# Attention, experts and feed-forward in one kernel: the parts of the row maxima move from VectorE to GpSimd in the plain attention stage

## The chip, the cores and the metric

One Trainium2 chip, one core. The metric is the device time of one execution in microseconds. The time of before is the median of three executions. One further execution was recorded by the hardware profiler; all rows below are from it.

## The reference

The kernel computes two layers on x of shape 8 x 512 x 256 with a context of the same shape, in this order (cut to what matters):

```python
x = x + L0_xattn(ctx, ctx, layernorm(x), mask, ...)   # 16 heads of 16, plain (mask only), then Wo
x = x + L0_ffn(layernorm(x), ...)                     # layer norm, causal attention of 16 heads, then
                                                      # 8 experts of 256 -> 1024 -> 256, the best 2 per token
x = x + L1_xattn(layernorm(x), ctx, ...)              # one head of 256, no mask
x = x + L1_ffn(layernorm(x), ...)                     # silu(gate) * up, integer weights times 1/127
```

In both attentions of 16 heads: scores = q k^T, p = softmax(scores), out = p v.

## The kernel before, in words

The work runs in seven phases with a barrier of all engines between them: `phase_first` (projections of the plain attention), `phase_attention` with causal False, `phase_second` (output projection, projections of the causal attention), `phase_attention` with causal True, the gates, the experts, and the last layer. The change touches the first four, one number in the experts' phase, and no arithmetic of the result.

`phase_attention` works on 32 units G: a batch has 16 heads, and a unit is four of them. Operands are split into a high and a low half of 16 bits, which share the contraction. For a unit, PE makes the scores once (`score`, L953), VectorE takes the row maxima from them (`top`, L1092, eight reductions a unit in the plain stage), and the negated maxima are added as further rows of the operands when PE makes the scores a second time, transposed (`shifted`, L975). ScalarE takes the exponent (L1072), PE weighs the values (`weigh`, L991), and VectorE divides (`normalise`, L1114 and L1116). The scores of unit G + 2 are made while unit G is in its second pass.

How the maxima reach the operands: VectorE makes their high and low parts in 16 bits (`shift`, L1103 and L1106), PE transposes them (`turn`, L1003, at step 8 of 16 of the unit before), ScalarE copies the row out (`shift_rows`, L1060), SyncE moves it into the operand with two DMAs (L885), and the unit's first product waits for these.

Heads are loaded by half batches (two units) into four slots; a load (`heads.load`, L189 and L191) is five DMAs, or four without a mask, and each half batch takes two loads. FIRST_LOADS = 2 half batches are loaded by the projection phases, the next two early in the attention ("late"), the others one load a unit.

Beside the plain attention, GpSimd splits 22 weight pieces (`prep`) into high and low halves: 16 of 2048 columns a lane, 3 of 512, 3 of 1536 (integers). Raw pieces and results have two buffers each. SyncE loads a raw piece (`raw_load`, L893) and stores a result (`pair_store`, L898); GpSimd scales (L867), takes the high half (L872) and the low half (L875). Ahead of the high half it waits for the store that last used the buffer:

```python
if i >= 2:
    pool.wait_ge(pair_out[i % 2], 16 * (i // 2))     # line 871
pool.tensor_copy(pair[:, HIGH], raw)                 # line 872
```

All DMAs of this phase are issued by SyncE in program order. Its turn G begins with the two rows of unit G + 1, for which it waits for ScalarE's copy; then come the late loads, the load of heads, the store of split G - 2 (line 919) and the raw load of split G (line 921). In the causal stage two of its turns load an expert's weights (L924) in two DMAs of 1 MB.

Of the kernel before, what the change touches and what calls it, by code (L numbers as in the profile page):

```python
# [12 lines left out]
ALU = mybir.AluOpType  # L13
# [4 lines left out]
P = 128  # L18
B, S, D = 8, 512, 256
TT = S // P  # L20
# [5 lines left out]
G_ALL = B * NG  # L26
EPS = 1e-5
NEG = -1e30
E_N, FF = 8, 1024
# [79 lines left out]
NSC = 1024.0  # L109
PRODUCTS = ((0, 0), (0, 1), (1, 0))  # L110
LOW, HIGH = 1, 0
# [81 lines left out]


LOADS0, LOADS1 = 10, 8
FIRST_LOADS = 2


def phase_first(nc, c, w, scr, vall, heads, pk, w16):
# [544 lines left out]
def phase_attention(nc, c, causal, scr, vall, oall, heads, extra, spare, prep):  # L744
# [3 lines left out]
    NP_BUF, NE, NM_BUF = 24 if causal else 12, 3, 4  # L748
    K6, Q6, ident, identh, idm, cmq, cmk = (heads.k, heads.q, heads.ident, heads.identh, heads.idm, heads.cmq,
                                            heads.cmk)  # L750
    nm = [c.sb(f"nm{s}", [P, TT, 2, 2]) for s in range(NM_BUF)]
    nparts = [c.sb(f"nparts{s}", [P, TT * 2, 2, 2], F16) for s in range(2)]
# [10 lines left out]
    qk, mask = scr["qk"], scr["mask"]  # L763
# [7 lines left out]
    if causal:  # L771
        masked = c.sem("masked")
    else:
        mask_set, pair_ready, prep_own = c.sem("mask_set"), c.sem("pair_ready"), c.sem("prep_own")
        raw_in, pair_out = ([c.sem(f"{n}{p}") for p in range(2)] for n in ("raw_in", "pair_out"))
        buffers = Arena(spare)
        raws = [buffers.take([P, 2048]) for _ in range(2)]
        prepared = [buffers.take([P, 2, 2048], F16) for _ in range(2)]
        assert len(prep) < G_ALL - 1

    def prob_of(unit):
        return prob[unit % NP_BUF // 4][:, unit % 4]
# [17 lines left out]
    NPAIR = len(pairs)  # L800
# [29 lines left out]
    with nc.Block() as block:  # L830

        @block.gpsimd
        def _(pool):
            if causal:
                for G in range(G_ALL):
                    for t in range(TT):
                        own = [k for k, u in enumerate(units) if u[0] == t]
                        heads_in, w = len(units[own[0]][1]), e_width(t)
                        at = (G * NU + own[0]) % NP_BUF
                        diagonal = (prob[at // 4][:, at % 4:at % 4 + len(own), 0:heads_in * w]  # L840
                                    .rearrange("p k (h n) -> p k h n", h=heads_in)[:, :, :, 0:P])
                        pool.wait_ge(p_ready, G * NU + own[-1] + 1)
                        pool.affine_select(out=diagonal, in_=diagonal, compare_op=ALU.is_ge, fill=0.0, base=0,  # L843
                                           pattern=[[0, len(own)], [0, heads_in], [1, P]], channel_multiplier=-1
                                           ).then_inc(masked, 1)
                return
            pool.memset(idm[:], 0.0).then_inc(mask_set, 1)
            pool.memset(cmq[:], 0.0).then_inc(mask_set, 1)
            pool.memset(cmk[:], 0.0).then_inc(mask_set, 1)
            pool.wait_ge(mask_set, 3)  # L850
            for v in range(3):
                at = (v - 1) * RT
                pool.affine_select(out=idm[:, v, :], in_=idm[:, v, :], compare_op=ALU.not_equal, fill=MC, base=at,
                                   pattern=[[-1, P]], channel_multiplier=1)
                pool.affine_select(out=cmq[:, v, :], in_=cmq[:, v, :], compare_op=ALU.is_ge, fill=-MC, base=at,
                                   pattern=[[-1, P]], channel_multiplier=1)
                pool.affine_select(out=cmk[:, v, :], in_=cmk[:, v, :], compare_op=ALU.is_ge, fill=-MC, base=-at,
                                   pattern=[[1, P]], channel_multiplier=-1)
            steps = 0
            for i, (src, n, dst, scale, integer) in enumerate(prep):  # L860
                raw, pair = raws[i % 2][:, 0:n], prepared[i % 2][:, :, 0:n]
                pool.wait_ge(raw_in[i % 2], 16 * (i // 2 + 1))
                if integer:
                    pool.tensor_copy(raw, raw.bitcast(I32)).then_inc(prep_own, 1)
                    steps += 1
                    pool.wait_ge(prep_own, steps)
                pool.tensor_scalar(raw, raw, scale, None, ALU.mult).then_inc(prep_own, 1)  # L867
                steps += 1
                pool.wait_ge(prep_own, steps)
                if i >= 2:  # L870
                    pool.wait_ge(pair_out[i % 2], 16 * (i // 2))
                pool.tensor_copy(pair[:, HIGH], raw).then_inc(prep_own, 1)  # L872
                steps += 1
                pool.wait_ge(prep_own, steps)
                pool.tensor_tensor(pair[:, LOW], raw, pair[:, HIGH], ALU.subtract).then_inc(pair_ready, 1)  # L875

        @block.sync
        def _(sp):
# [9 lines left out]
            def raw_load(i):  # L888
                src, n, dst, scale, integer = prep[i]
                if i >= 2:  # L890
                    sp.wait_ge(pair_ready, i - 1)
                raw = raws[i % 2][:, 0:n].rearrange("p (c f) -> p c f", c=src.shape[1])
                sp.dma_start(raw.bitcast(I32) if integer else raw, src).then_inc(raw_in[i % 2], 16)  # L893
# [11 lines left out]
            for G in range(G_ALL):  # L905
                if G + 1 < G_ALL:
                    shift_rows(G + 1)
                if G == 0:
                    heads.load(sp, *late[0], qk, mask)
                    heads.load(sp, *late[1], qk, mask)  # L910
                elif G <= 2:
                    heads.load(sp, *late[G + 1], qk, mask)
                if G >= 2 and G // 2 + SLOTS - 1 < NHB:
                    if G % 2 == 0:
                        sp.wait_ge(p_ready, G * NU)
                    heads.load(sp, G // 2 + SLOTS - 1, G % 2, qk, mask)
                if not causal:
                    if 2 <= G < len(prep) + 2:
                        pair_store(G - 2)
                    if 2 <= G < len(prep):  # L920
                        raw_load(G)
                elif G in (4, 6):
                    k = (G - 4) // 2
                    sp.dma_start(scr["ew_to"][:, 5, k], scr["ew"][5, k]).then_inc(scr["ew_in"], 16)  # L924
            if not causal:
                for p in range(2):
                    sp.wait_ge(pair_out[p], 16 * ((len(prep) + 1 - p) // 2))
# [151 lines left out]
        def _(dve):  # L1079
# [42 lines left out]
            for G in range(LA):  # L1122
                for p in range(NPAIR):
                    top(G, p)
                    if G == 1 and p < 2:
                        shift(0, p)
            for G in range(G_ALL):
                for p in range(NPAIR):
                    if G + LA < G_ALL:
                        top(G + LA, p)  # L1130
                    if p < 2 and G + 1 < G_ALL:
                        shift(G + 1, p)
                    if p == EARLY - 1 and G > 0:
                        normalise(G - 1)
# [359 lines left out]
def phase_experts(nc, c, scr, ew_to, ew_in, slots, hist, ones, xs_out):  # L1494
# [49 lines left out]
    with nc.Block() as block:  # L1544
# [173 lines left out]
        def _(pe):  # L1718
# [40 lines left out]
                    last.then_inc(y_ps, 1)  # L1759

            pe.wait_ge(map_ready, 2)
            pe.wait_ge(ew_in, 16 * 2 * E_N)
            transpose(0, 0)

            def expert_of(s):
# [817 lines left out]
```

## Time and profile before

| what | us |
|---|---|
| median of three executions | 2091.76 (2085.29 to 2096.83) |
| the profiled execution | 2095.28 |
| its span, first to last instruction | 2093.5 |
| PE busy in the span | 1770.4 |
| VectorE busy | 1332.8 |
| ScalarE busy | 1098.2 |
| GpSimd busy | 570.9 |

The span is what the profiler recorded between the first and the last instruction; the time of the execution is a little longer. A busy time is a sum over the whole span, and the phases have different limits, so shares are read by stretches. In the rows, PE is TensorE's matmul, PEld its weight load, DVE is VectorE, ACT ScalarE, POOL GpSimd, and SPq SyncE issuing a DMA. L1103 is line 1103 of the kernel before.

### The profile page before, as it was taken

To read this page: it belongs to the slowest core of one execution; us is meant where nothing else is said; L and a number is where in the kernel's file an instruction comes from. 1 tells how busy PE (TensorE), PEld (TensorE's weight loads), DVE (VectorE), ACT (ScalarE), POOL (GpSimd) and SP (SyncE) were. 2 spreads that over 40 slices of the span, in tenths; PEclk is the share of its full clock that TensorE was granted. 3 is DMA by queue.
4 is the path that set the end of the run, shared out by engine and by line. 5 is a ranking of instruction groups with operands and counts; after the bars stand their busy time and mean duration, and the time that the engine had idled before them with its cause. 6 is when DMAs were issued, how large, how long until landed. Compare 5 with 4: busy or idle time off the path is not lost. (4 is left out here: it accounts for less than half of the span.)

```text
span 2093.5 us, 40227 instructions
## 1 busy us (share of the span) xinstructions
PE 1770.4 (85%) x13889; PEld 1078.1 (51%) x13890; DVE 1332.8 (64%) x2426; ACT 1098.2 (52%) x2041; POOL 570.9 (27%) x479
## 2 busy tenths in 40 slices
PE   7668888999896889997675599999998469989987
PEld 4312222222673444444564488888887245556555
DVE  6478898996565668883575455555454367767753
ACT  6336777878452567775441244444443246546551
POOL 5244899510430223332366000000000422222000
PEclk9869999999997899998675799999999689999999
DMA  6524665410341121113322211111111411111000
GB/s 186 154 87 140 211 197 179 139 65 2 111 125 60 50 81 49 49 35 130 136 102 82 71 51 45 45 46 50 45 45 41 173 41 51 51 52 50 21 11 21
DMA packets 103208, 171.74 MB, mean 82 GB/s; under 512 B 16008, under 2 KB 78368, under 8 KB 98976
## 3 DMA queue, kind: packets, MB, share of 16 engines
q1 hardware_dynamic: 96928, 153.19, 22.9%
q0 software_dynamic: 6144, 16.79, 2.5%
q8 instruction: 80, 1.31, 0.3%
q14 instruction: 56, 0.46, 0.1%
HBM read 103.34 MB, written 61.87 MB: 79 GB/s over the span
## 5 line engine op out<-in xcount | busy, mean ns | idle before, releaser
L1092 DVE TENSOR_REDUCE a_nm<-a_psS 128x2 f32<-128x1024 f32 (+1 forms) x384 | 446.9, 1191 | 51.4 <-PE a_psS L953 38.3
L1072 ACT ACTIVATE a_prob<-a_psE 128x512 f32<-128x512 f32 (+2 forms) x660 | 335.2, 563 | 122.1 <-PE a_psE L975 120.5
L975 PE MATMUL a_psE<-wall 51*128 51x512 f16 (+3 forms) x1024 | 291.7, 359 | 38.1 <-DMA wall<-a_nrow 26.9
L953 PE MATMUL a_psS<-wall 49*128 49x512 f16 (+4 forms) x1024 | 268.2, 369 | 35.3 <-DVE a_nm L1092 22.6
L1710 ACT ACTIVATE ex_hf<-ex_psH,ex_b 128x256 f32<-128x256 f32 x312 | 130.7, 470 | 216.4 <-PE ex_psH L1741 216.4
L1741 PE MATMUL ex_psH<-ex_xT,wall 128*128 128x256 f16 x1872 | 232.1, 274 | 7.5 <-issue 4.1
L1755 PE MATMUL ex_psY<-wall,ex_hl 128*128 x1872 | 229.8, 273 | 1.4 <-DVEq L1661 0.4
L975 PEld LDWEIGHTS a_psE<-wall 51*128 51x128 f16 x1024 | 76.8, 95 | 276.1 <-ACT a_prob L1072 106.5
L1741 PEld LDWEIGHTS ex_psH<-ex_xT,wall 128*128 x1872 | 182.4, 98 | 34.7 <-issue 13.0
L1755 PEld LDWEIGHTS ex_psY<-wall,ex_hl 128*128 128x128 f16 x1872 | 179.3, 98 | 31.9 <-issue 10.9
L1672 DVE CAST ex_hl<-ex_hf 128x512 f16<-128x512 f32 x156 | 66.6, 427 | 182.2 <-ACT ex_hf L1710 180.4
L991 PE MATMUL a_psO<-a_prob,wall 128*32 128x512 f32 (+3 forms) x1576 | 171.2, 523 | 2.5 <-ACT a_prob L1072 0.7
L1072 ACT ACTIVATE wall<-a_psE 128x512 f32<-128x512 f32 x236 | 128.1, 604 | 42.7 <-PE a_psE L975 42.2
L1949 POOL MEMSET la_identh<- 128x128 f16 x1 | 0.2, 205 | 466.6 <-POOLq L2502 466.6
L867 POOL TENSOR_SCALAR xall<-xall 128x2048 f32<-128x2048 f32 (+2 forms) x22 | 102.6, 4664 | 72.7 <-DMA xall<-in_w 58.5
L843 POOL TENSOR_SCALAR_AFFINE_SELECT a_prob<-a_prob 128x512 f32<-128x512 f32 x112 | 73.5, 656 | 176.7 <-ACT a_prob L1072 176.6
L953 PEld LDWEIGHTS a_psS<-wall 49*128 49x128 f16 (+1 forms) x1024 | 70.6, 96 | 90.5 <-DVE a_nm L1092 57.8
L1673 DVE TENSOR_TENSOR ex_hl<-ex_hf,ex_hl 128x512 f16<-128x512 f32 x156 | 108.1, 693 | 5.4
L1088 DVE TENSOR_REDUCE a_nm<-a_psS 128x4 f32<-128x1024 f32 x64 | 61.2, 958 | 64.0 <-PE a_psS L961 64.0
L1972 POOL TENSOR_TENSOR la_var<-la_mv,la_eps 128x4 f32<-128x4 f32 x16 | 8.5, 533 | 315.2 <-DVE la_mv L2004 315.2
L961 PE MATMUL a_psS<-wall 64*128 64x128 f16 x1024 | 88.7, 229 | 0.0
L2336 PE MATMUL la_psG<-la_yT,la_wgate 128*128 128x512 f16 x288 | 72.5, 389 | 11.7 <-ACT la_yT L2215 11.7
(282 smaller groups left out, 3160.0 us busy)
## 6 DMA issues: line engine op xcount, KB each, us to landing
s_qk<-wall SPq DMA_DIRECT2D x32, 512.0 KB, 3.2
wall<-s_qk SPq DMA_DIRECT2D x128, 128.0 KB
xall<-in_w SPq DMA_DIRECT2D x16, 1024.0 KB, 11.8
s_ew<-xall SPq DMA_DIRECT2D x16, 1024.0 KB, 9.2
wall<-s_ew SPq DMA_DIRECT2D x16, 1024.0 KB, 10.6
ex_xt<-s_xs SPq DMA_DIRECT2D x39, 256.0 KB, 2.6
s_ys<-ex_yo SPq DMA_DIRECT2D x39, 256.0 KB, 2.2
t_xin<-in_x SPq DMA_DIRECT2D x16, 512.0 KB, 5.2
```

Of the source, the lines that this page charges most:

```text
L843: pool.affine_select(out=diagonal, in_=diagonal, compare_op=ALU.is_ge, fill=0.0, base=0, pattern=[[0, len(own)], [0, heads_in], [1, P]], c ...
L867: pool.tensor_scalar(raw, raw, scale, None, ALU.mult).then_inc(prep_own, 1)
L953: last = pe.matmul(psS[:, bank, col:col + n], Q6[s][at:at + SROWS, pr, t * P:(t + 1) * P], K6[s][at:at + SROWS, pr, 0:n], start=True, stop ...
L961: last = pe.matmul(psS[:, banks(use) + x, col + t * P:col + n], idm[at:at + RT, u + 1 - x, :], cmq[at:at + RT, u + 1 - x, :], start=False, ...
L975: last = pe.matmul(psE[unit % NE][:, col:col + w], K6[s][at:at + EROWS, pr, t * P:(t + 1) * P], Q6[s][at:at + EROWS, pr, S - w:S], start=T ...
L991: last = pe.matmul(psO[c4 * HP:(c4 + 1) * HP, S - w:S], vall[:, at:at + HP], prob_of(G * NU + k)[:, col:col + w], start=t == 0, stop=t == ...
L1072: act.activation(prob_of(unit)[:, 0:w], psE[unit % NE][:, 0:w], ACT.Exp, scale=ESC).then_inc(p_ready, 1)
L1092: dve.tensor_reduce(nm[G % NM_BUF][:, t, :, i], psS[:, at:at + 2, 0:n], axis=AX.X, op=ALU.max, negate=True).then_inc(s_free, 1)
L1673: dve.tensor_tensor(hl[q][:, 1, two, :], hf[:, two, :], hl[q][:, 0, two, :], ALU.subtract).then_inc(hl_ready, 1)
L1710: act.activation(hf[:, f, :], psH[f // 2][:, f % 2, :], ACT.Gelu_apprx_tanh, bias=b1[q][:, f:f + 1], scale=1.0 / (WSCALE * XSCALE)).then_i ...
L1741: last = pe.matmul(psH[f][:, j, :], ew_to[:, ds(e, 1), 0, wp, at:at + P].rearrange("p o f -> p (o f)"), xT[q][:, xp, d, :], start=n == 0, ...
L1755: last = pe.matmul(psY[t][:, 0:D], hl[q][:, hp, fc, t * P:(t + 1) * P], ew_to[:, ds(e, 1), 1, wp, fc * D:(fc + 1) * D].rearrange("p o d -> ...
```

## The change

In the plain stage the two instructions of `shift` leave VectorE. GpSimd makes the parts with three instructions (scale by 1/1024 into a new tile `nscaled`, copy to 16 bits, subtract), in the order parts of unit 0, then for each split i: parts of unit i + 1, split i; then the parts of the units left. The causal stage keeps `shift` on VectorE. FIRST_LOADS goes from 2 to 3, so that one half batch is loaded late in place of two: its two loads are issued in turns 0 and 1. The raw load of split G + 1 is issued in turn G, one turn earlier than before; the store of split G - 2 stays in turn G. In the causal stage the expert's weights are loaded in eight pieces of 256 KB, one a turn from 4 to 11, and the experts' phase waits for the new count.

```diff
-FIRST_LOADS = 2
+FIRST_LOADS = 3
...
             steps = 0
+
+            def shift_parts(G):
+                nonlocal steps
+                src = nm[G % NM_BUF][:].rearrange("p t x i -> p (t x) i")
+                dst = nparts[G % 2]
+                pool.wait_ge(s_free, (G + 1) * NPAIR)
+                pool.tensor_scalar(nscaled[:], src, 1.0 / NSC, None, ALU.mult).then_inc(prep_own, 1)
+                steps += 1
+                pool.wait_ge(prep_own, steps)
+                if G >= 2:
+                    pool.wait_ge(nT_ps, G - 1)
+                pool.tensor_copy(dst[:, :, HIGH], nscaled[:]).then_inc(prep_own, 1)
+                steps += 1
+                pool.wait_ge(prep_own, steps)
+                pool.tensor_tensor(dst[:, :, LOW], nscaled[:], dst[:, :, HIGH], ALU.subtract).then_inc(nparts_ready, 1)
+
+            shift_parts(0)
             for i, (src, n, dst, scale, integer) in enumerate(prep):
+                shift_parts(i + 1)
                 raw, pair = raws[i % 2][:, 0:n], prepared[i % 2][:, :, 0:n]
                 pool.wait_ge(raw_in[i % 2], 16 * (i // 2 + 1))
...
+            for G in range(len(prep) + 1, G_ALL):
+                shift_parts(G)
...
-                if G == 0:
-                    heads.load(sp, *late[0], qk, mask)
-                    heads.load(sp, *late[1], qk, mask)
-                elif G <= 2:
-                    heads.load(sp, *late[G + 1], qk, mask)
+                if G < len(late):
+                    heads.load(sp, *late[G], qk, mask)
...
                     if 2 <= G < len(prep) + 2:
                         pair_store(G - 2)
-                    if 2 <= G < len(prep):
-                        raw_load(G)
-                elif G in (4, 6):
-                    k = (G - 4) // 2
-                    sp.dma_start(scr["ew_to"][:, 5, k], scr["ew"][5, k]).then_inc(scr["ew_in"], 16)
+                    if 2 <= G + 1 < len(prep):
+                        raw_load(G + 1)
+                elif 4 <= G < 12:
+                    k, half, part = (G - 4) // 4, (G - 4) // 2 % 2, slice((G - 4) % 2 * 1024, (G - 4) % 2 * 1024 + 1024)
+                    sp.dma_start(scr["ew_to"][:, 5, k, half, part], scr["ew"][5, k, :, half, part]
+                                 ).then_inc(scr["ew_in"], 16)
...
-                    if G == 1 and p < 2:
+                    if causal and G == 1 and p < 2:
                         shift(0, p)
...
-                    if p < 2 and G + 1 < G_ALL:
+                    if causal and p < 2 and G + 1 < G_ALL:
                         shift(G + 1, p)
...
-            pe.wait_ge(ew_in, 16 * 2 * E_N)
+            pe.wait_ge(ew_in, 16 * (2 * (E_N - 1) + 8))
```

## Rows read from the trace of the kernel before

**Rows 1.** Busy time by stretch: start:end, length, busy of each engine, clock, DMA.
```profile
200.00:300.00 100.00, 85.33 (x595) 22.90 (x594) 90.96 (x101) 78.07 (x149) 91.80 (x25) 1.00 0.63 202
447.00:458.00 11.00, 10.60 (x77) 2.82 (x74) 10.40 (x13) 9.57 (x20) 0.00 (x0) 1.00 0.12 42
```

**Rows 2.** Timeline of ScalarE, row copies of the plain stage: start, length, instruction.
```profile
178.85 0.56 ACT L1060 COPY a_nrow<-a_psS 8x512 f16<-8x512 f16 x1
199.54 0.57 ACT L1060 COPY a_nrow<-a_psS 8x512 f16<-8x512 f16 x1 [0.89 <-PE a_psS L1003]
...
348.09 0.57 ACT L1060 COPY a_nrow<-a_psS 8x512 f16<-8x512 f16 x1 [0.88 <-PE a_psS L1003]
...
421.43 0.57 ACT L1060 COPY a_nrow<-a_psS 8x512 f16<-8x512 f16 x1 [0.40 <-PE a_psS L1003]
...
447.56 0.56 ACT L1060 COPY a_nrow<-a_psS 8x512 f16<-8x512 f16 x1
...
512.52 0.56 ACT L1060 COPY a_nrow<-a_psS 8x512 f16<-8x512 f16 x1
```

**Rows 3.** Timeline of VectorE: the high parts beside GpSimd's work, and without it.
```profile
232.59 2.29 DVE L1103 TENSOR_SCALAR a_nparts<-a_nm 128x16 f16<-128x16 f32 x1
...
465.83 0.16 DVE L1103 TENSOR_SCALAR a_nparts<-a_nm 128x16 f16<-128x16 f32 x1
```

**Rows 4.** Timeline of GpSimd: one split of 2048 columns, part of one of 512.
```profile
229.49 5.37 POOL L867 TENSOR_SCALAR xall<-xall 128x2048 f32<-128x2048 f32 x1 [1.56 <-DMA xall<-in_w]
234.92 1.93 POOL L872 CAST xall<-xall 128x2048 f16<-128x2048 f32 x1
236.93 4.08 POOL L875 TENSOR_TENSOR xall<-xall 128x2048 f16<-128x2048 f32 x1
...
365.12 0.61 POOL L872 CAST xall<-xall 128x512 f16<-128x512 f32 x1
365.81 1.16 POOL L875 TENSOR_TENSOR xall<-xall 128x512 f16<-128x512 f32 x1
```

**Rows 5.** Timeline of all engines: from a unit's transposes to the store.
```profile
236.28 0.39 PE L1003 MATMUL a_psS<-wall,a_nparts 128*8 128x128 f16 x4 [0.71 <-DVE a_nm L1092]
...
236.70 0.57 ACT L1060 COPY a_nrow<-a_psS 8x512 f16<-8x512 f16 x1 [0.50 <-PE a_psS L1003]
...
237.30 1.33 SPq L885 DMA_DIRECT2D wall<-a_nrow  x2
...
238.67 2.15 SPq L189 DMA_DIRECT2D wall<-s_qk  x4
...
241.54 0.44 SPq L898 DMA_DIRECT2D s_ew<-xall  x1
```

**Rows 6.** DMAs: landing of all 22 stores, one of 1 MB, those of 256 KB.
```profile
DMA to landing us min/median/max: 6.7/9.1/15.3
...
s_ew<-xall SPq DMA_DIRECT2D x1, 1024.0 KB, 10.8
...
s_lw<-xall SPq DMA_DIRECT2D x3, 256.0 KB, 6.9
```

**Rows 7.** Timelines of SyncE and GpSimd: the first raw loads and the first split.
```profile
133.28 0.92 SPq L893 DMA_DIRECT2D xall<-in_w  x2
...
138.36 5.39 POOL L867 TENSOR_SCALAR xall<-xall 128x2048 f32<-128x2048 f32 x1 [17.59 <-DMA xall<-in_w]
```

**Rows 8.** Busy time by stretch, behind a long wait; columns as in rows 1.
```profile
192.00:193.00 1.00, 1.00 (x8) 0.20 (x8) 1.00 (x2) 1.00 (x3) 1.00 (x1) 0.50 0.12 45
```

**Rows 9.** Timelines of ScalarE and PE in the causal stage: row copies, one wait.
```profile
681.34 0.57 ACT L1060 COPY a_nrow<-a_psS 8x512 f16<-8x512 f16 x1 [1.33 <-PE a_psS L1003]
...
721.11 0.39 PE L975 MATMUL a_psE<-wall 51*128 51x512 f16 x1 [4.00 <-DMA wall<-a_nrow]
...
770.23 0.57 ACT L1060 COPY a_nrow<-a_psS 8x512 f16<-8x512 f16 x1 [0.26 <-PE a_psS L1003]
778.80 0.57 ACT L1060 COPY a_nrow<-a_psS 8x512 f16<-8x512 f16 x1 [0.18 <-PE a_psS L1003]
```

More of the change, by code:

```diff
@@ L773, in phase_attention @@
     else:
+        nscaled = c.sb("nscaled", [P, TT * 2, 2])
         mask_set, pair_ready, prep_own = c.sem("mask_set"), c.sem("pair_ready"), c.sem("prep_own")
@@ L778, in phase_attention @@
         prepared = [buffers.take([P, 2, 2048], F16) for _ in range(2)]
-        assert len(prep) < G_ALL - 1
+        assert len(prep) < G_ALL - 3
     def prob_of(unit):
```

## The prediction

> **What bounds the kernel now.** I read the busy shares by stretch first, then the row copies of ScalarE as a clock of the units, then the timelines of one unit, and last the times to landing. The plain attention stage is about a fifth of the span. While GpSimd splits weights beside it, VectorE is 91% busy and GpSimd 92%; late in the stage, with GpSimd silent, PE is busy 10.60 of 11.00 us and VectorE 10.40 [rows 1]. One copy of a row (L1060) marks each unit: the last six steps are (512.52 - 447.56) / 6 = 10.83 us, while from 199.54 to 348.09 twelve steps take 12.38 us each, and one step takes 20.7 us [rows 2]. From 178.85 to 512.52 there are 27 steps in 333.7 us; at 10.83 they would take 292.4. So some 41 us lie above the floor that PE sets, and that is all the change can win here.
>
> A good part of the 41 us has a visible cause. L1103, which makes the high parts of the maxima on VectorE, takes 2.29 us at 232.59 and ends at 234.88, 0.02 us after GpSimd's L867 ends; with GpSimd silent it takes 0.16 us [rows 3, 4]. VectorE is held by GpSimd's long instructions.
>
> **The change, part by part: what VectorE loses.** Two instructions a unit, 0.33 us where nothing holds them, 2.5 us where L867 does [rows 3]. That is a gain only if nothing later takes its place, since without the hold the unit is PE's 10.83 us [rows 1, 2].
>
> **What GpSimd gets.** Three instructions a unit on 16 values a lane. No row shows them. From 512 to 2048 columns L872 grows from 0.61 to 1.93 us and L875 from 1.16 to 4.08, so both begin near 0.18 us [rows 4]; with 16 columns I take 0.22 each and 0.2 us for the gaps of three linked steps, 0.85 us a unit. The bounds are 0.5 (begin alone, no gaps) and 2.0 (each 0.61, as the dearest near row, with gaps); below nothing they can't be, as each is an instruction in the loop named next. A split of 2048 columns takes 11.52 us (229.49 to 241.01), so GpSimd alone needs 12.35 us a unit, already the pace of before.
>
> **What the order of GpSimd's work ties together.** This is the step that decides. Before, GpSimd's splits and the units of attention met nowhere. Now GpSimd runs parts(i+1), split i, parts(i+2), split i+1, and so on. Split i holds a wait that the diff leaves as it is: from i = 2 on, ahead of its L872, it waits until the store of split i-2 has landed (line 871), because that buffer is written again. SyncE issues that store in its turn G = i (line 919), after the shift rows of unit i+1, which wait for the row copy, which waits for the transposes, which wait for parts(i+1). So the store, which was 10 us ahead of need, is now issued only once parts(i+1) is made, and parts(i+2) can't be made until it has landed. Queued behind GpSimd's wait are its own L872, L875 and parts(i+2); waiting for those are PE's transposes of unit i+2 and with them everything of the attention.
>
> The price of one turn round this loop, from one unit of before [rows 5]: the transposes start, 0.42 us later the copy, 0.60 us later SyncE's first row; with 0.08 us for GpSimd's signal that is 1.10. From the first row to the store is 241.54 - 237.30 = 4.24 us, in which two rows, four head loads and a mask are issued. The store lands 9.1 us after issue, the median of 22, 16 of them of 1 MB and nearly all behind the same head loads [rows 6]. Then L872 and L875, 234.92 to 241.01, 6.09 us [rows 4], and the parts, 0.85. Sum 1.10 + 4.24 + 9.1 + 6.09 + 0.85 = 21.4 us a unit, against 12.4 before. Ends for the landing: 6.9 us (the stores of 256 KB) and 10.8 us (the slowest 1 MB store once the stage is running; the 15.3 was an early one, behind doubled head loads), so 19.2 to 23.1 us [rows 6]. I take 9.1, since the same transfers stand ahead of the store.
>
> The raw load goes out one turn earlier and is no shorter path: issued right behind the store, it is needed a whole turn later.
>
> **How many turns.** I number the row copies from 0 (178.85 is number 4, 199.54 number 5, 348.09 number 17, 421.43 number 23) [rows 2]. Copy i+2 follows copy i+1 by the loop of split i. Number 4 is late already, because the first looped store goes out after copy 3: GpSimd starts split 0 at 138.36, when its raw data is in [rows 7], and two splits with their parts later, 2 x 12.37, parts 3 are made at 163.1; copy 3 is then at about 165, the first looped store 4.8 us behind it, its landing 9 to 12 us, and 8.0 us for the rest, so 187 against 178.85. Splits 3 to 15: 13 x 21.4 = 278.2. Splits 16 and 17 have 512 columns (1.85 us in place of 6.09 [rows 4]) behind 1 MB stores: 2 x 17.2. Split 18 behind a 256 KB store: 15.0. Splits 19 and 20, 1536 columns (4.6 us, between the two) behind 6.9 us: 2 x 17.7. Split 21 behind 768 KB, 8.4 us between the two: 19.2 [rows 6]. Together 382.2, so copy 23 at 569 us against 421.43: 148 us late. The eight steps left take 8 x 10.83 = 86.6 against 91.1, with 1 us for a clock to recover: after a long wait PE was granted half its clock (0.50, that is 1.2 of 2.4 GHz) for some microseconds [rows 8]. The stage: 148 - 4.5 + 1 = +145 us. Inside the loop the half clock costs little, since PE has 21 us for work that takes 10.8.
>
> **Three half batches loaded early.** Both projection stages issue two more head loads (L189, 2.15 us and some 0.6 for a mask [rows 5]). The first lies in a queue that waits anyway, the last beside the landing of the final store; 0 to 1 us each, +1 in all. GpSimd's and SyncE's other steps aren't moved past.
>
> **The causal stage.** VectorE keeps its parts there. Its floor is 778.80 - 770.23 = 8.57 us a unit; from copy 681.34 to 770.23 there are eight steps in 88.9 us, 20.3 above the floor. Four waits of PE for a row that stood in the queue (the longest 4.00 us) come to 12.1, and what follows each wait is PE at less than full clock [rows 9]. Doubled head loads and two 1 MB loads of expert 5 stand ahead of those rows; after the change each turn has one head load, and the expert's 2 MB goes in eight pieces of 256 KB. Gain between 0 (the bytes are the same) and 20.3; I take 14, the waits and a little of their wake.
>
> **Sum.** The profiled execution took 2095.3 us (span 2093.5, with 1.8 around it), 3.5 above the median of 2091.8. 2095.3 + 145 + 1 - 14 = 2227 us.
>
> **The rivals.** (1) Slower by less, a short landing. The queue is emptier when units take longer, so the store may land as the first raw load did in an empty queue: issued at 133.28, used at 138.36, 5.1 us [rows 7]. The loop is then 17.4 us; 15 turns lose 4.0 each and the six short ones some 1.5: 2227 - 69 = 2158. Against it: the head loads are still issued 3 us ahead of every store, and a 256 KB store with them ahead still took 6.9. The Trainium skill, page "DMA: Bandwidth & Descriptors", section "Anatomy of one DMA — SWDGE (gpsimd) path", is on this rival's side: about 2.0 us plus the bytes over 436 GB/s, 4.4 us for 1 MB, by which the time would be an estimated 2140 us. It is given for another issue path, and the trace of before disagrees, with 9.1.
> (2) Faster, GpSimd's own pace. If the stores have landed whenever GpSimd reaches L872, the loop has no DMA in it, GpSimd needs 12.35 us a unit and VectorE's holds are gone. Parts 2 are made at 150.7 [rows 7], and copy 17 comes at 150.7 + 15 x 12.35 + 1.1 = 337 in place of 348, the three short splits run at 10.83, the three of 1536 at 11.05, the rest at 10.83: the last copy at 490 against 512.5, so 2095 - 23 - 14 + 1 = 2059. It decides if a store can land within about 5.4 us (L867) of the parts being made; the issue alone comes 5.3 us after them.
> (3) No difference: the parts are ready as early as before because GpSimd has room, the units stay at 12.4 us, and the causal gain is at its low end: 2085 to 2105. The 92% of GpSimd speaks against it [rows 1].
>
> **How the numbers follow.** Forecast (loop over the landing) 0.87; rival 1 0.05; rival 2 0.06; rival 3 0.02. Within the forecast the landing's ends move 15 turns by -33 or +26 us, GpSimd's small steps 21 turns by -7 or +24, and the causal stage by -6 or +14. All at one end would be 2181 to 2291; as the three don't hang together I take the landing's end with half of the others: 2187 to 2272. That leaves out the rivals, 0.13, and thin ends. Faster by over 0.5% 0.06, within 0.5% 0.02, slower 0.92; 0.5% is about what a measurement of this kernel can tell from no change.
>
> **What would show it.** Row copies of the plain stage some 21 us apart from number 4 to 17 and 10.8 from 24 on; GpSimd idle before L872 for about 9 us a unit, ended by the DMA of a store; no idle time of note before L867; PE waiting before L1003 for GpSimd, and its clock falling to half in each unit; VectorE's L1103 gone there, with reductions never over 1.3 us; the causal stage with 8.6 us steps from its fourth unit. GpSimd's three small steps near 0.85 us. The prediction is wrong if GpSimd is not idle before L872, or if copies come 12 to 15 us apart.

## The result, and the profile after

The changed kernel takes 2218.44 us (median of four runs, 2217.67 to 2218.91), the kernel before 2093.98 in the same comparison: a ratio of 1.060, 95% interval 1.057 to 1.064. The prediction said 2227, range 2187 to 2272, and slower. The profiled execution took 2218.91 us, its span is 2217.2 against 2093.5, so 123.7 us are to be found. A time below is the median of a kernel's executions on its chip, or its only one; some executions of a kernel take over 1.5% longer than its fastest, and the ratios, and the median of label e3_loads_alone, leave these out.

Timeline of ScalarE of the changed kernel, the row copies (now L1079): start, length, instruction, idle time before and what ended it. They answer to [rows 2].

```profile
167.01 0.56 ACT L1079 COPY a_nrow<-a_psS 8x512 f16<-8x512 f16 x1
188.63 0.57 ACT L1079 COPY a_nrow<-a_psS 8x512 f16<-8x512 f16 x1 [10.68 <-PE a_psS L1022]
...
470.88 0.57 ACT L1079 COPY a_nrow<-a_psS 8x512 f16<-8x512 f16 x1 [9.17 <-PE a_psS L1022]
...
576.07 0.57 ACT L1079 COPY a_nrow<-a_psS 8x512 f16<-8x512 f16 x1 [6.34 <-PE a_psS L1022]
...
642.24 0.56 ACT L1079 COPY a_nrow<-a_psS 8x512 f16<-8x512 f16 x1
653.07 0.56 ACT L1079 COPY a_nrow<-a_psS 8x512 f16<-8x512 f16 x1
663.89 0.56 ACT L1079 COPY a_nrow<-a_psS 8x512 f16<-8x512 f16 x1
```

The first two rows are copies 3 and 4, the third is copy 17, the fourth copy 23. From 4 to 17 thirteen steps take 282.25 us, 21.71 each, where twelve of the same steps took 12.4 each in [rows 2]; at the end the step is 10.82, as before. The units in between wait for GpSimd, and GpSimd waits for a DMA.

Timeline of GpSimd over one turn of the changed kernel (L867 to L875 are now the parts of the maxima; L886, L891 and L894 are the split's scaling, high and low halves).

```profile
274.86 5.36 POOL L886 TENSOR_SCALAR xall<-xall 128x2048 f32<-128x2048 f32 x1
289.53 1.89 POOL L891 CAST xall<-xall 128x2048 f16<-128x2048 f32 x1 [9.31 <-DMA s_ew<-xall]
291.51 4.05 POOL L894 TENSOR_TENSOR xall<-xall 128x2048 f16<-128x2048 f32 x1
295.53 0.25 POOL L867 TENSOR_SCALAR a_nscaled<-a_nm 128x16 f32<-128x16 f32 x1
295.85 0.20 POOL L872 CAST a_nparts<-a_nscaled 128x16 f16<-128x16 f32 x1
296.13 0.22 POOL L875 TENSOR_TENSOR a_nparts<-a_nscaled,a_nparts 128x16 f16<-128x16 f32 x1
```

Timelines of PE, ScalarE and SyncE over the same turn: transposes, row copy, rows, head loads, mask, store, raw load, and the next copy. They answer to [rows 5].

```profile
275.03 0.58 PE L1022 MATMUL a_psS<-wall,a_nparts 128*8 128x128 f16 x4 [9.29 <-POOL a_nparts L875]
...
275.65 0.57 ACT L1079 COPY a_nrow<-a_psS 8x512 f16<-8x512 f16 x1 [9.01 <-PE a_psS L1022]
...
276.25 1.33 SPq L906 DMA_DIRECT2D wall<-a_nrow  x2
277.62 2.15 SPq L189 DMA_DIRECT2D wall<-s_qk  x4
279.82 0.62 SPq L191 DMA_DIRECT2D wall<-s_mask  x1
280.49 0.44 SPq L919 DMA_DIRECT2D s_ew<-xall  x1
280.97 0.43 SPq L914 DMA_DIRECT2D xall<-in_w  x1
...
297.12 0.57 ACT L1079 COPY a_nrow<-a_psS 8x512 f16<-8x512 f16 x1 [9.29 <-PE a_psS L1022]
```

This is the loop, closed: copy at 275.65, first row 0.60 later, store 4.24 us after that, landed 9.04 us after its issue (289.53), 6.0 us of split, 0.82 us of parts, and 0.77 to the next copy at 297.12, 21.47 us after the last one. GpSimd stands for 9.31 us with an input that was ready.

Waits of the changed kernel in its plain stage (what was waited for: us in total, times, longest):

```profile
PE a_psS L1022 <- POOL a_nparts L875: 162.2, 20, 11.0
POOL xall L891 <- DMA s_ew<-xall: 154.6, 16, 13.2
```

Twenty waits of PE for GpSimd hold 162 us; 16 waits of GpSimd for a 1 MB store hold 155. The second makes the first.

Busy time by stretch of the changed kernel within the same turn (start:end, length, busy of PE, weight load, VectorE, ScalarE and GpSimd, clock, DMA share, GB/s); it answers to [rows 1, 8].

```profile
281.00:288.00 7.00, 5.84 (x43) 1.23 (x36) 6.73 (x6) 6.17 (x12) 0.00 (x0) 1.00 0.88 311
288.00:289.00 1.00, 0.00 (x0) 0.00 (x0) 0.22 (x1) 0.00 (x0) 0.00 (x0) 0.85 0.17 70
289.00:290.00 1.00, 0.00 (x0) 0.00 (x0) 0.00 (x0) 0.00 (x0) 0.47 (x1) 0.50 0.13 53
290.00:295.00 5.00, 0.00 (x0) 0.00 (x0) 0.00 (x0) 0.00 (x0) 4.91 (x2) 0.50 0.03 14
```

PE idles and is granted half its clock (0.50, 1.2 of 2.4 GHz) behind that. In the last microseconds before the store is in, all that moves has a DMA share of 0.13 to 0.17, what two to three of the 16 engines make up. That row became the best lead of the study.

Where the 123.7 us went, from first and last row copies of each stage: 2.3 up to the plain stage's first copy (131.25 to 133.53), 149.1 within that stage (381.3 to 530.4), 0.5 between the stages, -17.7 in the causal stage (286.3 to 268.6), and -10.5 behind it (1135.2 to 1124.7), in code that the change doesn't touch.

### The profile page after: what moved, and what is told of

Read it like the earlier page. It is cut to its first block and busy times, and to the rows that moved or that the text cites. A ratio compares the mean times of both kernels' runs of the same rounds, so it can differ in the third digit from the quotient of the medians.

```text
span 2217.2 us, 40269 instructions
## 1 busy us (share of the span) xinstructions
PE 1779.2 (80%) x13889; PEld 1077.5 (49%) x13890; DVE 1303.8 (59%) x2362; ACT 1094.1 (49%) x2041; POOL 589.5 (27%) x575
## 5 line engine op out<-in xcount | busy, mean ns | idle before, releaser
L1111 DVE TENSOR_REDUCE a_nm<-a_psS 128x2 f32<-128x1024 f32 (+1 forms) x384 | 438.9, 1174 | 59.8 <-PE a_psS L972 50.2
L972 PE MATMUL a_psS<-wall 49*128 49x512 f16 (+4 forms) x1024 | 283.5, 375 | 31.9 <-DVE a_nm L1111 15.6
L1774 PEld LDWEIGHTS ex_psY<-wall,ex_hl 128*128 128x128 f16 x1872 | 179.9, 98 | 31.2 <-issue 10.8
L1022 PE MATMUL a_psS<-wall,a_nparts 128*8 128x128 f16 x256 | 29.3, 248 | 174.2 <-POOL a_nparts L875 162.2
L1133 DVE RECIPROCAL a_rc<-a_psS 128x16 f32<-128x16 f32 x64 | 16.4, 256 | 212.0 <-PE a_psS L1030 212.0
L1079 ACT COPY a_nrow<-a_psS 8x512 f16<-8x512 f16 x64 | 36.5, 571 | 199.7 <-PE a_psS L1022 199.1
L1022 PEld LDWEIGHTS a_psS<-wall,a_nparts 128*8 128x8 f16 x256 | 15.7, 93 | 194.7 <-issue 172.6
L886 POOL TENSOR_SCALAR xall<-xall 128x2048 f32<-128x2048 f32 (+2 forms) x22 | 102.5, 4659 | 7.2 <-DMA xall<-in_w 6.7
## 6 DMA issues: line engine op xcount, KB each, us to landing
wall<-s_ew SPq DMA_DIRECT2D x14, 1024.0 KB, 10.2
```

The lines of the kernel that those rows point to most:

```text
L972: last = pe.matmul(psS[:, bank, col:col + n], Q6[s][at:at + SROWS, pr, t * P:(t + 1) * P], K6[s][at:at + SROWS, pr, 0:n], start=True, stop ...
L1111: dve.tensor_reduce(nm[G % NM_BUF][:, t, :, i], psS[:, at:at + 2, 0:n], axis=AX.X, op=ALU.max, negate=True).then_inc(s_free, 1)
L1774: last = pe.matmul(psY[t][:, 0:D], hl[q][:, hp, fc, t * P:(t + 1) * P], ew_to[:, ds(e, 1), 1, wp, fc * D:(fc + 1) * D].rearrange("p o d -> ...
```

## The experiments

My theory: the loop that the prediction describes sets the unit. Against it, (A) GpSimd simply has too much to do, and (B) the DMA queue is full, so that it matters little who waits for what. The first four kernels below, and the changed kernel with the head loads split, ran once each; they differ from the changed kernel (2217.67 to 2218.91 us) by 78 us and more.

**The store one turn earlier.** SyncE stores split G-1 in turn G, so nothing that GpSimd waits for hangs on the parts that it has just made.

```diff
-                    if 2 <= G < len(prep) + 2:
-                        pair_store(G - 2)
+                    if 1 <= G < len(prep) + 1:
+                        pair_store(G - 1)
```

> The changed kernel with one edit: the store of split G-1 is issued in turn G (before: of split G-2), so that the store which split i waits for goes out one row copy earlier. Theory (the loop over the landing of the store): the wait ahead of GpSimd's high half is gone, and the next late thing is the raw load: row copy to raw issue 5 us, landing 11, a split 11.5, parts 0.9, together some 29.6 us for two units, 14.8 a unit in place of 21.7; total about 2092 us (2080 to 2110), GpSimd idle before its scaling instead of before its high half. Rival A (GpSimd is simply too slow at the parts beside the splits): units stay near 21 us, total over 2190. Rival B (the rows wait in the DMA queue): unchanged within 20 us, since the same bytes are moved.

Measured 2097.75 us, within the range. Copies come in turn 12.3 to 13.7 and 16.0 to 17.7 us apart, some 15 in the mean. Timeline of GpSimd of this kernel, the scaling of one split, and its waits in the plain stage:

```profile
293.46 5.37 POOL L886 TENSOR_SCALAR xall<-xall 128x2048 f32<-128x2048 f32 x1 [5.50 <-DMA xall<-in_w]
```

```profile
POOL xall L886 <- DMA xall<-in_w: 42.5, 12, 8.3
```

No wait for a store is left, and 120 us are back. What is late next is the raw load, which lands 11.5 us after issue.

**Four result buffers in place of two.** No DMA changes its place; GpSimd waits for the store of split i-4 (the buffers and their counts go from two to four throughout; cut here to the wait).

```diff
-                if i >= 2:
-                    pool.wait_ge(pair_out[i % 2], 16 * (i // 2))
+                if i >= 4:
+                    pool.wait_ge(pair_out[i % 4], 16 * (i // 4))
...
```

> The changed kernel with four result buffers in place of two: split i waits for the store of split i-4, issued two turns earlier; no DMA is moved. Theory (loop over the landing): the same as with the store one turn earlier, 14.8 us a unit, total about 2092 us (2080 to 2110), within 10 us of that run. Rivals A and B: 2190 or more.

Measured 2096.09 us, steps of 16.2 and 13.4 us in turn. The same gain with every transfer where it was: it was the dependence that cost the time. The full queue (B) alone would have left the time where it was.

**Store and raw load ahead of the head loads.** The loop stays, the store's place changes.

```diff
                 if G + 1 < G_ALL:
                     shift_rows(G + 1)
+                if not causal:
+                    if 2 <= G < len(prep) + 2:
+                        pair_store(G - 2)
+                    if 2 <= G + 1 < len(prep):
+                        raw_load(G + 1)
                 if G < len(late):
                     heads.load(sp, *late[G], qk, mask)
...
-                if not causal:
-                    if 2 <= G < len(prep) + 2:
-                        pair_store(G - 2)
-                    if 2 <= G + 1 < len(prep):
-                        raw_load(G + 1)
```

> The changed kernel with SyncE's turn in another order: rows, store, raw load, and only then the loads of heads; the store stays in its turn. Theory (loop): the store is issued 2.8 us earlier in the loop and no head loads stand ahead of it, so that it lands in 5 to 7.5 us in place of 9.0; units of 15 to 17.5 us, total about 2100 us (2075 to 2150). If the landing does not depend on the head loads, units of 18.9 us and about 2162 us. Rivals A and B: no change.

Measured 2092.91 us, units of 14.2 to 14.8, a little under the 15 to 17.5 expected. DMAs of this kernel (transfer, count, KB each, median us from issue to landing):

```profile
s_ew<-xall SPq DMA_DIRECT2D x16, 1024.0 KB, 5.0
```

The landing falls from 9.1 to 5.0 us, with the raw load still issued right behind the store. So some 4 us of the landing belonged to what stood ahead. The Trainium skill, page "DMA: Bandwidth & Descriptors", section "Anatomy of one DMA — SWDGE (gpsimd) path", gives about 2.0 us plus the bytes over 436 GB/s for DMAs that GpSimd issues, an estimated 4.4 us for 1 MB. These stores are issued by SyncE, and the trace comes near that figure (5.0) only where no head load stands ahead of the store.

**The raw load one turn later,** as in the kernel before.

```diff
-                    if 2 <= G + 1 < len(prep):
-                        raw_load(G + 1)
+                    if 2 <= G < len(prep):
+                        raw_load(G)
```

> The changed kernel with the raw load of split G in turn G, as before the change. Theory (whatever SyncE issues behind a row copy and GpSimd needs before the next parts is in the loop): the raw load joins it: 1.4 us to the row, 4.7 to the raw load, landing 11, split 11.5, parts 0.9, some 29.4 us a unit in place of 21.7; total about 2360 us (2330 to 2385). Rival A: unchanged, 2218. Rival B: the queue is less crowded ahead of a row, unchanged or faster.

Measured 2360.66 us, units of 29.2 to 29.9. Timeline of GpSimd of this kernel:

```profile
274.76 5.36 POOL L886 TENSOR_SCALAR xall<-xall 128x2048 f32<-128x2048 f32 x1 [17.56 <-DMA xall<-in_w]
280.19 1.89 POOL L891 CAST xall<-xall 128x2048 f16<-128x2048 f32 x1
```

The loop now closes over the raw load, with all 11.5 us of a split behind it. The later store costs nothing there (no wait ahead of L891). A loop can be made longer as well as shorter by moving one transfer by one turn; neither A nor B has a reason for 29 us.

**The loads alone.** The kernel before with the early head loads and the pieces of 256 KB, the parts left to VectorE; and the early head loads without the pieces (the diff shows what both share; the pieces are those of the change).

```diff
-FIRST_LOADS = 2
+FIRST_LOADS = 3
...
-                if G == 0:
-                    heads.load(sp, *late[0], qk, mask)
-                    heads.load(sp, *late[1], qk, mask)
-                elif G <= 2:
-                    heads.load(sp, *late[G + 1], qk, mask)
+                if G < len(late):
+                    heads.load(sp, *late[G], qk, mask)
```

> The kernel before with only the loads of the change: three half batches loaded early, one late, the expert's weights in eight pieces; the parts stay on VectorE, raw loads and stores in their old turns. Theory (everything lost is in the loop, and the loads are a gain by themselves): causal stage 17.7 us shorter as in the changed kernel, the long step of 20.7 us in the plain stage about 8 shorter, the projection stages 2.5 longer: 23 us under the kernel before, about 2069 us (2060 to 2082). Rival (the loads only moved waiting about): within 5 us of before.

> The kernel before with three half batches loaded early and nothing else; the expert's weights stay two loads of 1 MB. Theory: the two waits of the causal stage behind doubled head loads go, the two behind the expert's loads and their wake, 8.8 us, stay: some 14 us under before, about 2078 us (2068 to 2088), and 9 us over the run with both. Rival (the head loads alone made all four waits): the same as the run with both.

Measured, each against the kernel before on its chip (2094.64 us): both 2071.22 us (ratio 0.988, 0.983 to 0.993), early loads only 2071.47 (0.987, 0.980 to 0.994). So the 9 us that were expected between the two don't show in the totals. The causal stage of the profiled runs tells the parts apart, between its first and last row copy: 286.3 us before, 276.1 with the early loads, 268.5 with the pieces too, 268.6 in the changed kernel. So the -17.7 us are -10.2 from the early loads and -7.6 from the pieces, and none from the parts. The profiled run with both loses again what the pieces gain: its plain stage took 383.4 us, against 373.0 with the early loads only, though the program of that stage is the same in the two, and 381.3 before. Neither is near the 530.4 of the changed kernel, so the 149 us of the plain stage come from the parts on GpSimd and their order, not from the head loads.

**Both repairs.** The store a turn earlier and ahead of the head loads: the first and third edits together.

> The changed kernel with both repairs: the store of split G-1 in turn G, and the rows, the store and the raw load ahead of the head loads. Theory: no DMA is left in the loop, as the raw load lands 10 us behind the row copy and GpSimd needs 12.3 us for its own instructions; units at GpSimd's pace, 12.4 us from copy 3 to 17, no more: about 2058 us (2045 to 2070). Rival (VectorE's or PE's 10.8 us is reached at once): 2035 or less. Rival (the loop has another member): units over 13.5 us, 2075 or more.

Measured 2049.0 us, ratio 0.976 (0.969 to 0.982). Copies come 12.1 to 12.8 us apart, and GpSimd waits for no store; its waits for raw loads come to 5.9 us in the whole stage. Timeline of GpSimd of this kernel, one whole unit:

```profile
291.27 0.25 POOL L867 TENSOR_SCALAR a_nscaled<-a_nm 128x16 f32<-128x16 f32 x1
291.59 0.20 POOL L872 CAST a_nparts<-a_nscaled 128x16 f16<-128x16 f32 x1
291.88 0.22 POOL L875 TENSOR_TENSOR a_nparts<-a_nscaled,a_nparts 128x16 f16<-128x16 f32 x1
292.06 5.37 POOL L886 TENSOR_SCALAR xall<-xall 128x2048 f32<-128x2048 f32 x1
297.50 1.89 POOL L891 CAST xall<-xall 128x2048 f16<-128x2048 f32 x1
299.48 4.08 POOL L894 TENSOR_TENSOR xall<-xall 128x2048 f16<-128x2048 f32 x1
303.53 0.25 POOL L867 TENSOR_SCALAR a_nscaled<-a_nm 128x16 f32<-128x16 f32 x1
```

303.53 - 291.27 = 12.26 us without a gap: here A is true. GpSimd's own pace is the bound once the loop is cut, 12.26 us and not 21.7.

**GpSimd's work spread out.** The splits' instructions are no longer one split a unit: between two parts go as many of them as fit into 9.8 us, in a list made beforehand, and there are three raw buffers.

```diff
-            shift_parts(0)
-            for i, (src, n, dst, scale, integer) in enumerate(prep):
-                shift_parts(i + 1)
...
+            shift_parts(0)
+            for g in range(G_ALL):
+                if g + 1 < G_ALL:
+                    shift_parts(g + 1)
+                for i, q in chunks[g]:
...
```

> The run with both repairs, and GpSimd's splits spread over the units: behind each unit's parts only as many of a split's instructions as fit 9.8 us (two of three, mostly), with three raw buffers, loads and stores in the turns that this gives. Theory: GpSimd needs at most 10.5 us a unit, less than PE's 10.83, so the units come at PE's pace from copy 2 on, no step over 11.5 us but at the start; last row copy of the plain stage near 473 us, total about 2034 us (2026 to 2048). Rival (GpSimd and the DMAs cost VectorE or PE something beside the order of waits): units over 11.5 us, 2055 or more.

Measured 2042.91 us, ratio 0.973 (0.966 to 0.979). The total is within the range, but the units are not as expected: many take 10.8 us, others up to 15.3, where no step over 11.5 was expected. Timeline of PE of this kernel within the longest, and its busy time by stretch around it (columns as above):

```profile
299.54 0.60 PE L1044 MATMUL a_psE<-wall 51*128 51x512 f16 x1 [2.63 <-DMA wall<-a_nrow]
```

```profile
292.00:297.00 5.00, 4.66 (x34) 1.10 (x31) 4.54 (x6) 3.85 (x9) 5.00 (x2) 1.00 0.20 63
297.00:302.00 5.00, 2.46 (x14) 0.53 (x14) 1.94 (x3) 2.11 (x4) 1.59 (x3) 0.65 0.19 62
302.00:308.00 6.00, 5.87 (x38) 1.51 (x32) 4.30 (x5) 4.18 (x9) 5.83 (x4) 0.72 0.04 13
```

PE waits for the unit's rows, two loads of 4 KB issued at 292.61, while the DMA engines move 62 GB/s at a share of 0.19. Most of the 16 engines idle while PE waits: the queue is slow, not full. Over the stage, PE's waits for such rows come to 17.9 us, in 12 turns.

**Doubled head loads as two.** That pointed at the head loads. Of the four DMAs of one load (without the mask), two read 16 rows and write them twice, as 2 x 16 rows (L189). "Doubled" means these here; in the prediction and in the expectation of label e7_early_only it means two loads issued in one turn. The edit issues each of these as two loads of 16 rows; the bytes stay the same, 128 KB (the expectation below has 256 KB, which is wrong).

```diff
-                if hi - lo > HD:
-                    run = run.unsqueeze(0).to_broadcast([2, HD, GH * S])
-                sp.dma_start(tile[at + lo:at + hi].rearrange("p h n -> p (h n)"), run).then_inc(self.in_[s], 16)
+                for row in range(lo, hi, HD):
+                    sp.dma_start(tile[at + row:at + row + HD].rearrange("p h n -> p (h n)"), run).then_inc(self.in_[s], 16)
...
-LOADS0, LOADS1 = 10, 8
+LOADS0, LOADS1 = 14, 12
```

In the changed kernel:

> The changed kernel with one edit: each doubled head load (256 KB to 32 rows from 16, read twice) goes as two loads of 16 rows, six DMAs a half batch in place of four; the same bytes in the same place of the queue, and SyncE issues some 1.1 us longer a turn. Theory T (the store lands late because the doubled loads ahead of it run on two of the 16 DMA engines; in the changed kernel the DMA share is 0.13 at 53 GB/s in the last microsecond before the store of unit 8 is in, so two engines finish last): the store lands in 5.0 to 5.6 us, as where nothing stood ahead of it, so a unit of the loop takes 21.7 - 9.0 + 5.3 + 1.1 = 19.1 us; 14 of these turns and 6 short ones at some 3 us less each give 2219 - 54 = about 2165 (2150 to 2175). Theory U (it is the bytes ahead, on however many engines): the landing stays near 9 us and SyncE's longer turn is added to the loop, 22.8 us a unit: about 2240.

In the kernel with GpSimd's work spread out:

> The kernel with GpSimd's steps spread over the units (label e9_spread), with the doubled head loads as two loads of 16 rows each. There PE still waited 17.9 us in 12 turns for rows of the maxima that stood in the queues behind head loads and a raw load (2.63 us at 299.54, and half the clock granted behind it). Theory T (two slow engines): the rows land sooner, the waits and their wake go, and the plain stage comes from 356.5 between its first and last row copy towards 31 x 10.83 = 336: 345, so 2043 - 11 = 2032 us (2024 to 2038). Theory U (bytes): no gain, 2043 to 2050, the rows 1 us later by SyncE's longer turns.

In the kernel before:

> The kernel before, with the doubled head loads as two loads of 16 rows each and nothing else. Theory T: in the causal stage the rows stand behind doubled head loads on two engines, so four of the waits of the kernel before (12.1 us in all) and their wake go: 286 to about 272 us there; in the plain stage VectorE, held by GpSimd, sets the pace and little is gained, 0 to 6 us: about 2094 - 17 = 2077 us (2066 to 2086). Theory U: within 0.5% of the kernel before.

Measured 2140.15, 2016.01 and 2048.36 us; the last two against 2095.05 us of before on their chip: 0.962 (0.958 to 0.966) and 0.977 (0.971 to 0.983). Busy time by stretch, first of the kernel before, then of the kernel before with this edit, each late in the plain stage, where one load of heads is all that is loaded (issued from 449.5 and from 447.8):

```profile
450.00:451.00 1.00, 0.75 (x8) 0.19 (x3) 0.69 (x2) 0.92 (x2) 0.00 (x0) 1.00 0.24 70
...
454.00:455.00 1.00, 1.00 (x13) 0.21 (x5) 1.00 (x1) 0.67 (x3) 0.00 (x0) 1.00 0.12 45
455.00:456.00 1.00, 0.92 (x7) 0.19 (x4) 1.00 (x3) 1.00 (x3) 0.00 (x0) 1.00 0.14 57
456.00:457.00 1.00, 1.00 (x9) 0.16 (x10) 1.00 (x3) 1.00 (x3) 0.00 (x0) 1.00 0.12 46
```

```profile
449.00:450.00 1.00, 0.96 (x10) 0.25 (x10) 1.00 (x2) 1.00 (x3) 0.00 (x0) 1.00 0.49 164
450.00:451.00 1.00, 1.00 (x9) 0.21 (x5) 1.00 (x1) 0.67 (x2) 0.00 (x0) 1.00 0.55 131
451.00:452.00 1.00, 1.00 (x8) 0.35 (x11) 0.96 (x2) 1.00 (x3) 0.00 (x0) 1.00 0.31 69
452.00:453.00 1.00, 1.00 (x12) 0.13 (x5) 1.00 (x2) 0.85 (x2) 0.00 (x0) 1.00 0.00 1
```

As doubled loads they are still running 7 us after the first issue, at a share of 0.12, two engines of 16, and some 50 GB/s; as loads of 16 rows they are done by 452, within 1 us of the mask that is issued behind them. The Trainium skill, page "DMA: Bandwidth & Descriptors", section "Why a DMA increments its semaphore by 16 and not by 1", has the rule: a DMA runs on the largest number of engines, up to 16, that divides the slowest dimension on both sides, so [2, 16, ...] runs on two and [16, ...] on all. The traces agree: 0.12 is 2/16. Why a store behind such a load is late then reads so: the store has shares of its own on those two engines, and is in only when they are. That step is argued; the landings, with such loads ahead and without, are what the runs show.

In the changed kernel the 1 MB stores now land in 5.0 us where 9.1 stood. DMAs of this kernel (columns as above), and its timelines of GpSimd and SyncE:

```profile
s_ew<-xall SPq DMA_DIRECT2D x16, 1024.0 KB, 5.0
```

```profile
277.36 1.89 POOL L890 CAST xall<-xall 128x2048 f16<-128x2048 f32 x1 [6.39 <-DMA s_ew<-xall]
```

```profile
267.01 1.29 SPq L905 DMA_DIRECT2D wall<-a_nrow  x2
268.35 3.06 SPq L188 DMA_DIRECT2D wall<-s_qk  x6
271.44 0.63 SPq L190 DMA_DIRECT2D wall<-s_mask  x1
272.12 0.45 SPq L918 DMA_DIRECT2D s_ew<-xall  x1
```

The store of this turn lands after 277.36 - 272.12 = 5.24 us, and the units from copy 3 to 17 take 17.7 to 19.0 us, mostly 18.1 to 18.5 (19.1 expected). Theory U falls in all three kernels: the bytes are the same, and all three are faster. But all three totals also lie below the ranges of theory T (2150, 2024 and 2066 us at their low ends), in part because I had left out the start: the first row copy comes at 120 to 123 us in place of 131 to 134. The 8 to 11 us lie in the first projection stage, which issues head loads between its own transfers; PE's waits there for VectorE's copy of the values come to 9.6 to 9.9 us in these three kernels, against 18.4 in the kernel before and 19.0 in the changed one. In the causal stage the split loads alone give 268.5 us on the kernel before, as much as the early loads and the pieces together gave. There PE's waits for rows fall from 13.5 us in five to 1.4 in one, though the expert's loads of 1 MB stand ahead of the rows as before.

With everything together every unit of the plain stage from its third step on takes 10.8 us: from first to last copy 459.15 - 122.63 = 336.5 us, where 31 x 10.83 is 335.7. PE no longer waits for rows there, where 17.9 us stood. Busy time by stretch of that kernel, which answers to the first row of [rows 1]:

```profile
200.00:300.00 100.00, 95.60 (x667) 25.39 (x664) 93.05 (x93) 85.57 (x166) 76.05 (x47) 1.00 0.57 166
```

PE is busy 95.6 of 100 us, where [rows 1] has 85.3; GpSimd 76. This kernel beats both, 2016 us against 2094 and 2218.

## Why the prediction was right

The step that decided it, the loop over the store's landing, held in place, mechanism and size.

- **The loop:** 21.4 us a unit forecast, 21.71 measured over 13 units, and each link as put down: from the parts to the first row 1.37 (1.10), rows to store 4.24 (4.24), landing 9.04 (9.1), split 6.0 (6.09), parts 0.82 (0.85). Of the 0.27 us more in the first link, 0.20 are PE at half its clock (transposes 0.58 us against 0.39 in [rows 5]); "costs little" was right, but I had put nothing for it into the sum.
- **The short splits:** 17.4, 17.3, 14.9, 18.7, 17.5 and 19.3 us against 17.2, 17.2, 15.0, 17.7, 17.7 and 19.2. Copy 4 at 188.6 (187), copy 23 at 576.1 (569): 4.1 in the 13 long turns, 1.6 up to copy 4 and 1.2 in the short splits make the 7 us.
- **GpSimd's small steps** were the unknown price, bounded at 0.5 to 2.0: three instructions of 0.25, 0.20 and 0.22 us. Taking the lower rows as nearest was right: [rows 4], extrapolated from 512 and 2048 columns to 16, gives an estimated 0.18 us for the copy and 0.22 for the subtraction; the scaling has one size there only.
- **The raw load** was no shorter path, as said. It is the next one in line: 11.5 us, and it bounds the unit at about 15 us as soon as the store doesn't.
- **The landing's cause** was half seen. "The same transfers stand ahead" was right, and the reason why the short landing was refused; but the prediction doesn't say what in those transfers delays the store. It is the loads on two engines of 16. The first rival's landing (5.1 us) is real, 5.0 to 5.2, and appears once those loads are split or stand behind; an emptier queue, the rival's own reason, did not bring it.
- **The second rival,** GpSimd's own pace of 12.35 us, was no fiction either: 12.26 with the store earlier and first, and 2049 us where it said 2059.
- **Three half batches early:** +1 forecast, +2.3 at the start and +0.5 between the stages. SyncE issues the last early load until 117.6 us, where it was done at 100.8, and PE's first scores start at 119.66 in place of 117.22.
- **The causal stage:** -14 forecast, -17.7 measured, within 0 to 20.3, and 8.6 us a unit from the third step on. PE's waits for rows, of which [rows 9] shows the longest, came to 12.1 us by the prediction's count, and to 1.7 in the whole changed kernel; so their wake was worth more than "a little".
- **The end** was not in the sum: -10.5 us behind the causal stage, in work that no edit touches. Over the thirteen traces of this study this stretch lasts 1123 to 1135 us, longest in the four kernels with the parts on VectorE (1130 to 1135) and 1123 to 1128 in the others. Most of it stands in one place of the last layer: in those four VectorE stands for 7.8 to 8.2 us ahead of one reduction and waits for nothing that the profile shows ("issue"), and in the other nine it doesn't. The line of the kernel before, from its timeline of VectorE:

```profile
1866.82 0.69 DVE L2066 TENSOR_REDUCE la_top<-la_psU 128x1 f32<-128x512 f32 x1 [7.75 <-issue]
```

What VectorE lacks there is not shown. Without the end the sum of measured terms is 2095.3 + 149.1 + 2.8 - 17.7 = 2229.5.

Of what the prediction wanted to see, all stood there: GpSimd idle some 9 us ahead of the high halves (L891), none before L886 in this turn, half the clock behind each wait, and 10.8 us steps from copy 24 on. The total lies 8.6 us under the forecast, and the end, which nothing forecast, is more than all of that; the terms that were worked out miss by +4.1, +1.8 and -3.7 us, which nearly cancel.

## What to carry to other kernels

Before a small step is put between the long ones of another engine, write down what that engine waits for and go back along each wait: if one of them is issued behind the step's own result, a path that had slack becomes a loop, and its length, DMA landing included, is the new time of a turn. Cut the loop (an earlier issue, another buffer) before counting what the step saves, then fit the long steps into the gaps. And where a transfer lands late, look at the DMA share while it is late: a small share with work queued is not a full queue, and here it was a transfer that runs on few engines.

## What the runs showed of the hardware

- A load whose outermost dimension is 2 moves at some 50 GB/s at a DMA share of 0.12, and 1 MB issued behind two of them and their two single ones lands in 9.0 us, against 5.0 where the same bytes are loaded with an outermost dimension of 16. Two more DMAs a load cost SyncE 0.9 us (3.06 against 2.15).
- The kernel before was bound by this as well: the split loads alone take it from 2095.05 to 2048.36 us, 11 us of it at the start and 18 in the causal stage by the profiled run, which at 2063 us is the slowest of its four (2037 to 2063); where the faster ones gain more is not shown.
- GpSimd's instructions on 16 columns take 0.20 to 0.25 us, with gaps of 0.07 us between linked ones.
